# Rebuilding the last two attention periods of a fused attention, mixture-of-experts and zone kernel

## The reference, cut to what matters

```
    x = x + attn(cond(x, cond_1024, weight), w_qkv, w_out)
    x = x + ffn(cond2(x, cond_1024, W_router, router_bias, s_w1, s_w3, s_w2, r_w1, r_w2), W1, b1, W2, b2, Wa, Wb)
attn:  scores = einsum('bhsd,bhtd->bhst', rope(q), rope(k)) / sqrt(8), causal
       attn = softmax(scores); out = einsum('bhst,bhtd->bhsd', attn, v); return out @ w_out.T
cond2: shared = sum over 2 experts of (silu(x @ s_w1.T) * (x @ s_w3.T)) @ s_w2.T, halved
       s = sigmoid(concat(x, t) @ W_router.T); idx = top_k(s + router_bias, 2)
       routed = sum over 8 experts of gelu(x @ r_w1.T) @ r_w2.T * gates; return (shared + routed) / 4
ffn:   x + sum over the 3 chosen zones of gelu(x @ Wa[e]) @ Wb[e] * w[e]
```

## Time and profile before

| what | us |
|---|---|
| median of the runs (180.86 to 181.63) | 181.37 |
| the profiled execution | 180.98 |
| its span, first to last instruction | 179.1 |
| the rest of it, outside the span | 1.88 |
| PE busy | 168.9 (94%) |
| DVE busy | 138.9 (78%) |
| ACT busy | 134.3 (75%) |
| POOL busy | 93.8 (52%) |

### The profile page before, as it was taken

One profiled execution on the slowest core, in us unless ns is written; L12 is line 12 of the kernel. 1 busy time (PEld: TensorE's weight loads), 2 busy tenths in 40 slices (PEclk: granted clock), 3 DMA queues, 4 the chain that ended last, 5 costly groups with the idle time before them and its releaser, 6 DMA issues.

```text
span 179.1 us, 3278 instructions
## 1 busy us (share of the span) xinstructions
PE 168.9 (94%) x943; PEld 116.8 (65%) x944; DVE 138.9 (78%) x444; ACT 134.3 (75%) x224; POOL 93.8 (52%) x117
## 2 busy tenths in 40 slices
PE   6899999899999999988999999996999989999992
PEld 2656575565666666653758767864687867788881
DVE  5588989989898899980586999699799658637551
ACT  3569177688768888889734787953879999999970
POOL 5508088985463969688532522021769931676000
PEclk9999999999999999999999999999999999999999
DMA  4824775676686567520110899960760000001001
GB/s 144 294 46 107 191 203 159 218 234 213 166 267 208 143 194 194 164 94 5 62 51 17 231 345 344 347 178 4 241 230 0 0 4 0 0 2 59 0 4 59
DMA packets 15349, 24.28 MB, mean 136 GB/s; under 512 B 2844, under 2 KB 4828, under 8 KB 15308
## 3 DMA queue, kind: packets, MB, share of 16 engines
q1 hardware_dynamic: 14532, 23.29, 42.2%
q10 hardware_dynamic: 800, 0.79, 1.7%
HBM read 18.71 MB, written 5.27 MB: 134 GB/s over the span
## 4 chain that ended last, share of the span: by engine, by line
PE 70%; DVE 11%; ACT 7%; issue 6%; POOL 4%; DVEq 0%; ACTq 0%; POOLq 0%
PE psum L1407 11%; PE psum L1540 10%; PE psum L1541 9%; PE psum L1542 9%; PE psum L1467 8%; PE psum L1443 7%; PE psum L1286 3%; PE psum L1338 2%; PE psum L1352 2%; ACT t_probs L1105 2%; DVE psum L772 2%; DVE t_raw L924 1%; PE psum L1402 1%; ACT t_q_pad L1155 1%; PE psum L1447 1%
## 5 line engine op out<-in xcount | busy, mean ns | idle before, releaser
L772 DVE CUSTOM_DVE_ANT_0 psum<-psum,t_causal 128x128 f32<-128x128 f32 (+3 forms) x128 | 58.6, 525 | 5.8 <-PE psum L1407 3.0
L1105 ACT ACTIVATE t_probs<-psum 128x1024 f32<-128x1024 f32 (+2 forms) x48 | 40.9, 883 | 8.2 <-PE psum L1443 5.2
L1407 PE MATMUL psum<-t_stacked,t_q_pad 96*128 96x256 f32 (+2 forms) x104 | 33.3, 391 | 0.5 <-DVE t_row_max L772 0.2
L1407 PEld LDWEIGHTS psum<-t_stacked,t_q_pad 96*128 96x128 f32 x104 | 18.4, 189 | 12.4 <-DVE t_row_max L772 10.2
L672 POOL TENSOR_SCALAR_AFFINE_SELECT t_probs<-t_probs 128x512 f32<-128x512 f32 x32 | 20.5, 651 | 9.0 <-ACT t_probs L1105 9.0
L944 DVE SCALAR_TENSOR_TENSOR t_q_pad<-psum,t_zw_all,t_q_pad 128x512 fp32r<-128x512 f32 x24 | 17.8, 748 | 9.3 <-ACT t_q_pad L1153 9.2
L1139 ACT ACTIVATE psum<-psum 128x512 f32<-128x512 f32 x40 | 23.4, 586 | 0.9 <-PE psum L1542 0.3
L703 POOL TENSOR_TENSOR t_q_pad<-t_raw,t_q_pad 128x512 fp32r<-128x512 f32 x8 | 10.8, 1357 | 21.0 <-ACT t_q_pad L1155 21.0
L1467 PE MATMUL psum<-t_probs,t_v_all 128*32 128x512 f32 (+3 forms) x256 | 20.6, 439 | 0.0
L772 DVE DVE_READ_ACCUMULATOR2_ANT t_row_max<- 128x1 f32 x128 | 18.0, 141 | 0.0
L1153 ACT ACTIVATE t_q_pad<-psum,t_zw_all 128x512 fp32r<-128x512 f32 x24 | 16.5, 688 | 1.2 <-PE psum L1542 0.6
(11 more groups left out here) (233 smaller groups left out, 369.6 us busy)
## 6 DMA issues: line engine op xcount, KB each, us to landing
t_stacked<-scratch SPq DMA_DIRECT2D x16, 256.0 KB, 5.7
t_probs<-in_L_ffn_Wa SPq DMA_DIRECT2D x2, 1024.0 KB, 11.5
scratch<-t_o_sb SPq DMA_DIRECT2D x7, 256.0 KB, 2.1
t_raw<-in_experts SPq DMA_DIRECT2D x7, 256.0 KB, 3.6
t_stacked<-scratch SPq DMA_DIRECT2D x9, 192.0 KB, 3.7
t_q_pad<-scratch SPq DMA_DIRECT2D x28, 48.0 KB
scratch<-t_dn_hi SPq DMA_DIRECT2D x2, 512.0 KB, 3.4
t_q_two<-scratch SPq DMA_DIRECT2D x5, 192.0 KB, 2.6
```

Of the source, the lines that this page charges most:

```text
L772: last = V.tensor_tensor_reduce(scores, scores, causal[:, S - width:S], 1.0, 3 * BIG, ALU.add, ALU.max, row_max[s][:, qb, j:j + 1])
L1105: A.activation(o, scores, ACT.Exp, scale=float(1.0 / np.sqrt(np.float32(HD)))).then_inc(exp_done, 1)
L1407: last = T.matmul(bank[:, o:o + width], q_pad[s][0:TOP, j, qb * P:(qb + 1) * P], stacked[0:TOP, n, 0:width], start=True, stop=True)
```

## The change

Four things are edited, in the tables and on all five engines.

1. The expert weights are prepared a period earlier: the seven splits move from (3,0) to (6,0) to (2,0) to (5,0), and the loads become three in entry 1, three in entry 2 and one in entry 3. Where a load stands in its entry, and where a split stands in its period, is unchanged.
2. `normalise(0)` leaves DVE; POOL does the same multiplication in period 5, behind the spreading of the last queries.
3. PE calls `project_out(0)` and `lay_max_under_q(7)` in period 6 ahead of score tile 4, with two banks of the ring for them; `place_max(7)` moves to c = 0 of POOL's period 6; the copy of the laid rows goes from ACT to DVE (`copy_last_qm`), behind `residual(0)`.
4. Period 7 of PE is written out: routing stands behind the second score tile, the `weigh_v` parts of group 6 between the other tiles, `up(0)` behind the sixth tile, and all four parts of group 7's `weigh_v` behind it. ACT takes the exponent of the logits behind exp(7,1). DVE's `take_outputs(6)` moves from ahead of `residual(0)` to between parts 1 and 2 of the gates.

```diff
...
 RING_ORDER += [("max", 1, _u) for _u in range(2)] + [("lay", 0)] + [("max", 1, _u) for _u in range(2, FIRST)]
 for _n in range(GROUPS):
     RING_ORDER += [("max", *_u) for _i in range(SLICES) for _u in max_units(_n, _i)]
-RING_ORDER += [("out", 0), ("route", 0)]
+RING_ORDER += [("out", 0), ("lay", GROUPS - 1)]
+LAST = GROUPS - 1
 AT = {
     "normalise 1": [3],
...
 }
-INV_AT = [(6, 8), (7, 10)]
-SPLITS = {(3, 0): 0, (3, 2): 1, (4, 0): 2, (4, 2): 3, (5, 0): 4, (5, 2): 5, (6, 0): 6}
-EXPERT_LOADS = [(), (0, 1), (2, 3), (4, 5), (6,), (), (), ()]
+INV_AT = (6, 8)
+SPLITS = {(2, 0): 0, (2, 2): 1, (3, 0): 2, (3, 2): 3, (4, 0): 4, (4, 2): 5, (5, 0): 6}
+EXPERT_LOADS = [(), (0, 1, 2), (3, 4, 5), (6,), (), (), (), ()]
 WARM = 8
...
         def qm_bank(n):
-            return ST[:, slot_of("exp", n - 1, STU - 1) + 1, :] if n else ring("lay", 0)
+            return ST[:, slot_of("exp", n - 1, STU - 1) + 1, :] if 0 < n < LAST else ring("lay", n)
         def ring(*item):
...
                 for c in range(3):
                     pool.wait_ge(exp_done, STU * n + 2 * c + 2)
-                    if c == 1 and n + 1 < GROUPS:
+                    if c == 1 and n + 1 < LAST:
                         place_max(n + 1)
                     for o in ((0,) if c < 2 else (0, 2 * P)):
                         tri = probs[n % 2][:, c, :, o:o + P]
                         last = G.affine_select(out=tri, in_=tri, compare_op=ALU.is_ge, fill=0.0, base=0,
                                                pattern=[[0, HG], [1, P]], channel_multiplier=-1)
                     last.then_inc(masked, 1)
+                    if c == 0 and n + 1 == LAST:
+                        place_max(LAST)
                     if c == 2 and n + 1 < GROUPS:
                         spread_last_queries(n + 1)
+                    if c == 2 and n + 2 == LAST:
+                        pool.wait_ge(packed, 32)
+                        G.tensor_tensor(packed_out[:], packed_out[:], packed_sum[:], ALU.mult).then_inc(onorm_ready, 1)
                     if n == 0 and c == 0:
                         turn(1)
                     if n == 0 and c == 1:
...
                 dve.wait_ge(pv_full, n + 1)
                 dve.wait_ge(stored[n % 2], 16 * (n // 2))
                 V.tensor_copy(o_sb[n % 2][:], PV).then_inc(pv_copied, 1)
+            def copy_last_qm():
+                dve.wait_ge(qm_full, GROUPS)
+                V.tensor_copy(q_mov[LAST % BUFS][TOP:ROWS, :], qm_bank(LAST)[TOP:ROWS, :]).then_inc(qm_copied, 1)
             def x1_high(b):
...
                 reduce_max(n, u)
                 if (n, u + 1) == (0, len(MX_UNITS[0])):
                     place_first_max()
-                if (n, u) == INV_AT[0]:
+                if (n, u) == INV_AT:
                     invert(0)
-                if (n, u) == INV_AT[1]:
-                    normalise(0)
             dve.wait_ge(ld_small, 16)
             dve.wait_ge(mx_reduced, len(MX_LIST))
             for b in range(B):
                 V.tensor_copy(temb[:, b, :], cond[:, b:b + 1].broadcast_to([P, P])).then_inc(temb_ready, 1)
-            take_outputs(GROUPS - 2)
             residual(0)
+            copy_last_qm()
             x1_high(0)
             x1_low(0)
             dve.wait_ge(w_lo, len(range(0, UP_COLS, S)) + len(range(0, DN_COLS, S)))
             gates(0, 0)
             gates(0, 1)
+            take_outputs(LAST - 1)
             gates(0, 2)
             gates(0, 3)
             invert(1)
...
             def exp_of_minus_logits(b):
                 act.wait_ge(logits, b + 1)
-                bank = (ring("route", 0) if b == 0 else MISC)[:, 0:KB * EXPERTS]
+                bank = (MISC if b else QM)[:, 0:KB * EXPERTS]
                 A.activation(e_neg[b], bank.rearrange("p (t e) -> p t e", t=KB), ACT.Exp,
                              scale=-1.0).then_inc(expneg, 1)
...
                 if n == 1:
                     take_hi(1)
                 exp(n, 1)
+                if n == LAST:
+                    exp_of_minus_logits(0)
                 if 0 < n < GROUPS - 1:
                     copy_pv(n - 1)
                 exp(n, 2)
...
                 exp(n, 4)
                 if n == 0:
                     take_hi(0)
-                if n + 1 < GROUPS:
+                if n + 1 < LAST:
                     copy_qm(n + 1)
-                if n == GROUPS - 1:
-                    exp_of_minus_logits(0)
                 exp(n, 5)
                 if (n, 2) in SPLITS:
                     split_high(SPLITS[n, 2])
...
             def lay_max_under_q(n):
                 pe.wait_ge(m_ready, n + 1)
-                if n:
+                if 0 < n < LAST:
                     wait_slot("exp", n - 1, STU - 1)
                 else:
-                    wait_ring("lay", 0)
+                    wait_ring("lay", n)
                 if n == 0:
                     pe.wait_ge(const_ready, 1)
                 for qb in range(KB):
...
                 pe.wait_ge(temb_ready, B)
                 pe.wait_ge(x1_ready, b + 1)
                 if b == 0:
-                    wait_ring("route", 0)
-                bank = ring("route", 0) if b == 0 else MISC
+                    pe.wait_ge(qm_copied, GROUPS)
+                bank = MISC if b else QM
                 T.matmul(bank[:, 0:KB * EXPERTS], temb[:, b, :], small[:, W_RT:W_RB], start=True, stop=True)
                 for t in range(KB):
                     last = T.matmul(bank[:, t * EXPERTS:(t + 1) * EXPERTS],
...
                 kind, b, w = UNITS[i]
                 r = i % RING
                 if i == 0:
-                    pe.wait_ge(expneg, 1)
+                    pe.wait_ge(mx_reduced, len(MX_LIST))
+                    pe.wait_ge(x1_ready, 1)
                     pe.wait_ge(w_lo, (UP_COLS + DN_COLS) // S)
                 elif i < RING:
                     pe.wait_ge(exp_done, GROUPS * STU)
...
                 T.matmul(MISC[:, 80:80 + TOPZ], ones_row[:], zw[:, b, :], start=True, stop=True).then_inc(z_bc, 1)
-            for n in range(GROUPS):
+            for n in range(LAST):
                 def maximum(i):
                     for unit in max_units(n, i):
...
                     weigh_v(n - 1, 3, 3 * P, S)
                 maximum(3)
                 scores_for_exp(n, 2)
-                if n == GROUPS - 1:
+                scores_for_exp(n, 3)
+                if n + 1 == LAST:
                     project_out(0)
-                scores_for_exp(n, 3)
+                    lay_max_under_q(LAST)
                 maximum(4)
                 maximum(5)
                 maximum(6)
                 scores_for_exp(n, 4)
-                if n == GROUPS - 1:
-                    route_experts(0)
+                if n + 1 == LAST:
+                    scores_for_exp(n, 5)
                 weigh_v(n, 0, 0, S)
-                maximum(7)
-                if n + 1 < GROUPS:
+                if n + 1 < LAST:
+                    maximum(7)
                     lay_max_under_q(n + 1)
-                maximum(8)
-                scores_for_exp(n, 5)
-                maximum(9)
-                maximum(10)
+                    maximum(8)
+                    scores_for_exp(n, 5)
+                    maximum(9)
+                    maximum(10)
+            scores_for_exp(LAST, 0)
+            scores_for_exp(LAST, 1)
+            route_experts(0)
+            scores_for_exp(LAST, 2)
+            weigh_v(LAST - 1, 1, P, S)
+            scores_for_exp(LAST, 3)
+            scores_for_exp(LAST, 4)
+            weigh_v(LAST - 1, 2, 2 * P, S)
+            weigh_v(LAST - 1, 3, 3 * P, S)
+            scores_for_exp(LAST, 5)
             up(0)
-            weigh_v(GROUPS - 1, 1, P, S)
-            weigh_v(GROUPS - 1, 2, 2 * P, S)
-            weigh_v(GROUPS - 1, 3, 3 * P, S)
+            weigh_v(LAST, 0, 0, S)
+            weigh_v(LAST, 1, P, S)
+            weigh_v(LAST, 2, 2 * P, S)
+            weigh_v(LAST, 3, 3 * P, S)
             for i in range(1, N_UNITS + LAG):
```

## The result

| | before | after |
|---|---|---|
| median of the runs, us | 181.41 | 188.58 (186.92 to 189.81) |
| ratio, 95% interval | | 1.037 [1.029, 1.045] |
| profiled execution, us | 180.98 | 187.63 |
| its span and mean granted clock | 179.1, 1.000 | 185.7, 0.991 |

The changed kernel is 7.2 us slower by the medians and 6.6 by the profiled executions. I had forecast 2.3 with a range up to 185.4, so the sign was right and the time was outside the range. Times of before here are those of its runs beside each kernel (181.26 to 181.41 by median).

The account below looks back on a forecast made before the run. PE was taken to bound the kernel (70% of the chain). +3.7 us in period 2 less 1.4 in the tail made +2.3: 183.3 for the profiled execution, 183.7 for the median, range 182.2 to 185.4.

Parts of the forecast that it names:

- the tail: End of the kernel, periods 6 and 7 onward: forecast to give back 1.4 us, bounds 1.0 to 1.7.
- part 4: Period 7 reordered: up(1) on PE 1.7 us earlier, DVE's second inversion 1.4 earlier; the later one, DVE, sets the gain.
- Part 1: Splits a period earlier: ACT waits 4.0 us for chunk 0's load in period 2, delaying PE's laying 3.7 (2.3 to 4.2).
- rival (c): Periods 3 to 5 pay the gap back through fewer PE waits for DVE, up to 4 us; 180.0 with 3.7; chance 0.06.
- Rival (d): ACT doesn't stand at the load in period 2, for instance because it lands within 1 us; 180.0; chance 0.03.
- Rival (b): The clock falls to 1.2 GHz in PE's 3.7 us gap in period 2, adding 1.5 us: 185.2; chance 0.13.
- my own signs of being wrong: First split doesn't wait, periods behind it are shorter than 8.24 us, or the granted clock leaves 1.00 there.
- Part 2: Normalise on POOL: DVE's 0.69 us goes; POOL's 1.28 us multiplication ends 0.25 before PE's projection, costing nothing.
- Part 3: Projection and laying in period 6: laying at 80.7 after a 0.4 us gap; tiles 0 and 1 end at 83.65, before 84.45.
- (a): The tail gives nothing back, a later store, gather or multiplication ending as late as the old chain: 185.1; chance 0.13.

Follow-up runs that it names:

- e2: The kernel before with only the change's new SPLITS and EXPERT_LOADS tables, its tail left old: 187.12 us (1.034 of before).
- e3: e2 plus 16 matmuls, results unread, in PE's gap ahead of the laying of period 2: 184.77 us (1.020 of before).
- e1: The changed kernel with the old SPLITS and EXPERT_LOADS tables, its new tail kept: 183.72 us (1.013 of before).
- e6: The changed kernel with expert chunk 0 loaded one table entry earlier, in period 1: 182.49 us (1.002 of before).
- e8: e6 with DVE's invert(1) moved behind its products of the second expert unit: 180.85 us (0.997 of before).
- e9: e6 with ACT instead of DVE copying group 6's outputs, behind exp(7,4), and invert(1) behind the first unit's products: 180.69 us (0.995 of before).
- e13: The changed kernel with its 8 warming matmuls of 512 columns at the start made 32 of 128, results unread: 189.08 us median.

## Why the prediction was wrong

The account of the profiled executions, forecast 183.3, measured 187.6: start-up +0.56, clock +1.41, and the tail +1.0 instead of -1.4, together 4.4 where 4.3 are missing. By medians the miss is 4.9; the further 0.6 is the spread of four runs, which the clock doesn't explain (the run of 186.92 has 0.982, that of 189.53 has 0.990). Two terms failed: the clock, which the sum put at nothing, and the landing of the store in part 4.

- **Part 1, the standing at the load: right.** 3.7 forecast, 3.63 measured; the split started at 51.54, and less the 0.56 of the start-up that is 50.98 (51.1 forecast). The landing of the same load in the kernel before, 4.4, was the right row: it was 4.29. Nothing was paid back later, so rival (c) fell: periods 4 and 5 took 8.21 and 8.24. Rival (d) fell with the 3.81.
- **Rival (b), the clock: it happened, and the sum had no term for it.** I had priced it at +1.5 and it was +1.41 in the profile (1.48 between those of e2 and e3, 2.35 between their medians). The price was right and the chance of 0.13 was not; a granted clock that leaves 1.00 was among my own signs of being wrong. What I had for evidence was one gap of 1.62 us at clock 1.00, and I let it stand against a gap over twice as long. It bore on neither side. The Trainium skill (TensorE: Matmul & The Clock Gate, HAM oscillation — how this bites in real kernels), which the prediction cites for this rival, has such gaps put the clock back. The trace agrees, 0.50 behind a gap of 3.50 us, and I gave the page too little weight.
- **Part 2, normalise on POOL: right.** It took 1.28 and PE did not wait for it. That its cover hangs on the earlier splits was not said; e1 shows what it costs without them, PE's 1.05 us at the laying.
- **Part 3: right within 0.2.** The laying on before's clock is at 80.7 as forecast, PE's gap 0.21 where I had 0.4.
- **Part 4: the step that failed.** PE's side came as forecast: up(1) at 92.1 for 91.85, the first gate step at 85.7 for 85.5. The chain of the sums failed in one term: the store took 3.71 instead of the 2.0 of the earlier trace rows. The gather took 2.45, where I had 1.9 and an upper bound of 2.3. So the sums came 2.4 us later than forecast, and DVE's gain of 1.4 became a loss of 1.0. I had bounds for the gather, but for the store I had only its own earlier landing, as if a transfer kept its duration when it moves in time. The packet was there to be seen in the trace of before, at 89.2, 0.8 us behind the store's data (to 88.4), and my own sum moved the store from 86.7 to 89.35, so its data to about 90.2 to 91.1, and PE's packet with PE. That a store of this kernel can take 4.4 was there, too, at 73.32. Where exactly the two would meet no row of before shows.
- **The range** held (a) and (b) singly. They are independent, one in period 2 and one in the tail, and with both it is 181.37 + 3.7 + 1.5 = 186.6. Rival (a) itself was cut off at no gain, with no case in which the tail loses.

## What to carry to other kernels

Before work that waits for a load is moved forward, look at where that load is issued: here one table entry (e6) decided between 7.2 us lost and about 1 (0.3 by the ratio). An in-order engine that stands in front of a transfer should have other ready work put before the wait (e8, e9), since the landing of one transfer differed here by a factor of two with what happened to pass beside it. And independent rivals are to be added up when the range is drawn.

## What the runs showed of the hardware

- A gap of 3.50, 3.67 and 3.84 us on PE (the kernel after, e2, e13) was followed by 3.4 us with a granted clock of 0.50, which began 0.6 to 1.3 us after PE had started again; one of 1.62 us was not the earlier trace rows, nor was the same stretch filled with matmuls (e3). What lies between 1.62 and 3.5 no run shows. It cost 1.4 to 1.5 us in the profiles, on top of the standing.
- A 16 KB block of PE's instructions moves on the DMA engines that also carry the kernel's transfers, for 0.9 to 1.7 us on one of them, and nine packets of a 256 KB store beside it waited for its end: the store landed after 3.4 to 4.4 us instead of 2.0. Adding 24 matmuls 70 us earlier moved the block away.
- So an edit that adds or removes instructions shifts DMA times elsewhere: 24 small matmuls in time that was idle anyway took 1.6 us off the landing of e9's store of group 6 and put 1.4 on that of an earlier store; the time of the kernel did not get better for it (180.61 to 180.93 by trimmed medians, within the spread). The runs of the kernels with the new tail spread more than those of before (e6 from 180.7 to 183.8 with one at 185.8); why is open.
